# Four weight loads re-timed, one product moved and two statistics handed to ScalarE in a fused attention and expert layer

## The chip, the cores and the metric

The kernel runs on one core of a Trainium2 chip. The metric is the time of one execution in microseconds (us) on the device; lower is better. A core has TensorE (PE, with its weight loads shown apart as PEld), VectorE (DVE), ScalarE (ACT), GpSimd (POOL) and SyncE (SP), which run their own instruction streams and wait for each other by semaphores, and 16 DMA engines that SP and POOL feed here.

## The reference

Input `x` is 4 sequences of 1024 tokens with 256 features, float32. The layer is attention and then a routed feed-forward, each on a normalized input and added to its own input:

```python
qkv = layernorm(x) @ qkv_w.T + qkv_b            # 16 heads of 16, rope on q and k
attn = softmax(causal(q k^T / 4)); x = x + (attn @ v) @ proj_w.T + proj_b
z = layernorm(x)
aff = z @ centroids.T; e = argmax(aff)          # 8 experts, top 1 for each token
ye = z + relu(layernorm_e(z) @ w1[e].T + b1[e]) @ w2[e].T + b2[e]
alpha = sigmoid(aff[e]); x = x + alpha * ye + (1 - alpha) * z
```

Each expert has a first weight matrix of 1024 x 256 and a second of 256 x 1024, 1 MB each.

## The kernel before

The program has three stages.

**Projection** (0 to about 120 us) makes q, k and v and writes q and k as bfloat16 parts to DRAM (`qk_parts`).

**Attention** (about 120 to 523 us) runs in 16 steps, n = 0 to 15, one for each group of four heads of a sequence (`NQ`), and a short tail. In step n, PE computes the scores and products of group n (L1252, L1269) and, between them at hand-written places (`ITEM_AT`, `PV_AT`), 18 "items" of group n+1 (L1145, L1156), from which DVE takes block maxima (L1009). The first item of a step (`item == 0`) waits until the whole stack of q and k of its group is in SBUF: 14 DMAs, `STACK_LOADS`, which SP issues in `load_stack` (L387, L392, L396, L401) for group n+2 in the second half of step n, and which are complete on one semaphore. Ahead of them in each step, in SP's program order, SP stores the inverted softmax sums of an earlier group (`store_inverse`, L228), places an output (`place_out`, L213, L217), sends the maxima (L744) and spreads inverted sums (`spread_inverse`, L235). In step 5, 7 and 9 it then stores three pad rows. Once in some steps, at sub-step `W2_AT = 4`, POOL issues one load of 1 MB from its own queue: the second weights of one of the first `LOADED = 6` experts (L824). `early_at` says in which step each goes.

**Route and experts** (from 523 us). For `NP = 16` pairs of token tiles PE projects the attention output (L2049, L2053), DVE adds the residual and keeps the logits (`add`, L1673, L1674), and mean and variance of the pair are taken either by DVE (`stats` of DVE, L1683, L1686) or by ACT (`stats` of ACT, L1564, L1568, L1570), as `BY_ACT` says. Pairs are grouped (`GROUPS`); per group DVE finds the expert (`one_hot`), PE makes ranks (`rank_products`), DVE makes row positions (`positions`, `row_scalars`), and POOL scatters the rows of the group's tiles to DRAM by one indirect DMA for each tile (L1506). After group 3 the first slot table is made. SP, in its own order, loads x, the columns and the biases, then waits until all attention outputs are normalized (`s_nm`) and loads the second weights of experts 6 and 7 (L1460, 2 MB), then waits for the slot table and loads the first weights of slot 0 (L246), then waits for the scatters of groups 0 to 3 (L1465) and loads the rows of slots 0 and 1 (L344):

```python
for e in range(LOADED, NE):
    if e == OUT_AT_WEIGHTS:
        sp.wait_ge(s_pj, KB)
    if e == INV_AT_WEIGHTS:
        sp.wait_ge(s_nm, NQ // 2)
    sp.dma_start(w2s[:, e * W2C:(e + 1) * W2C], w_exp[e][:, W1C:WCOLS]).then_inc(s_late, 16)
sp.wait_ge(s_tab, 2)
load_w1(sp, Step(0))
```

The attention outputs are normalized in 8 products of 128x1024 (`normalize_out`, L242): six on POOL, two on DVE. The last of them is in DVE's pair loop. PE waits for it before pair 12. Then 39 slots (32 full, 7 of half size) follow, each a hidden layer (L2075) and an output (L2099); the first needs its rows normalized by ACT (L1557) and turned by PE (L1996), the register loads of three slots (L1426) and the projection of pair 15, which PE does between them.

Of the kernel before, what the change touches and what calls it, by code (L numbers as in the profile page):

```python
# [45 lines left out]
FIRST_GROUPS = 4  # L46
# [84 lines left out]
def program(nc, x, x_feat, w_qkv, b_qk, b_val, w_proj, w_proj_out, b_proj, cent, w_exp, cols, b2, consts, rope, out):  # L131
    ctx = ExitStack()
    with ctx:
# [229 lines left out]
        def wait_rows(eng, S):  # L363
# [3 lines left out]
            else:  # L367
                wait_dma(eng, s_rl, S)

        phase_route_experts(nc, x, pay_d, load_w1, load_rows, load_half_rows, row_data, row_scalar, wait_rows, w2s, w1b, s_w1, cols, b2, cst, ident, eps, slot_tab, col, b2r,  # L370
                            wp, bp3, ones3, xl, o_feat, arena[:, spare:NE * WCOLS], arena[:, spare - 2 * W2C:spare], s_b3, out, gate,
                            o_late[:, 0, :], w_exp, s_late, s_nm, place_out, invert_sums, store_inverse, spread_inverse, normalize_out)
# [34 lines left out]
def phase_project_attend(nc, x, x_feat, w_qkv, b_qk, consts, rope, parts_d, w_exp, s_w, arena, v_all, spare, cst, ident, eps,  # L407
# [5 lines left out]
    with ExitStack() as ctx:  # L413
# [238 lines left out]
        def wait_free(eng, i, item, alone=None):  # L652
            wait(eng, s_free, i, ITEMS, number(i, item) + 1, alone)

        early_at = (1, 2, 3, 4, 5, 14)
        W2_AT = 4
        assert len(early_at) == LOADED
        BY_POOL = NQ // 2 - 2
# [630 lines left out]
def phase_route_experts(nc, x, pay_d, load_w1, load_rows, load_half_rows, row_data, row_scalar, wait_rows, w2s, w1b, s_w1, cols, b2, cst, ident, eps, slot_tab, col, b2r,  # L1289
# [3 lines left out]
    with ExitStack() as ctx:  # L1293
# [12 lines left out]
        starts = [sum(GROUPS[:g]) for g in range(NG + 1)]  # L1306
        FIRST = GROUPS[:FIRST_GROUPS]
        FT = sum(FIRST)
        BY_ACT = range(1, 2 * FIRST_GROUPS, 2)

        def pairs_by(act, u):

            return sum((m in BY_ACT) == act for m in range(u))

# [113 lines left out]
        def expert_of(eng, S, known):  # L1428

            if S.reg is not None:  # L1430
                return expert(eng, S)
            if S.const not in known:
                known[S.const] = expert(eng, S)
            return known[S.const]
# [5 lines left out]
        with nc.Block() as block:  # L1440
# [99 lines left out]
            def _(act):  # L1540
                known = {}

                def roots(g):
                    act.wait_ge(s_v, 2 * pairs_by(False, starts[g + 1] // 2))
                    act.wait_ge(s_va, 5 * pairs_by(True, starts[g + 1] // 2))
                    act.activation(sd[:, 0, of(g)], mv[:, of(g), 1], ACT.Sqrt, bias=eps).then_inc(s_sd, 1)
                    if g == 0:
                        act.wait_ge(s_pre, 6)
                    act.activation(sd[:, 1, of(g)], mv[:, of(g), 1], ACT.Sqrt, bias=eps2[:, :], scale=1.0 + EPS).then_inc(s_sd, 1)
# [10 lines left out]
                def stats(u):  # L1560
                    before = pairs_by(True, u)
                    act.wait_ge(s_x2, u + 1)
                    for t in (2 * u, 2 * u + 1):
                        act.activation(junk[:, t % 2, :], xr[:, t, 0:DIM], ACT.Copy, scale=1.0 / (HD * DIM),  # L1564
                                       accum_out=am[:, t:t + 1]).then_inc(s_va, 1)
                    act.wait_ge(s_va, 5 * before + 2)
                    for t in (2 * u, 2 * u + 1):
                        act.activation(junk[:, 2 + t % 2, :], xr[:, t, 0:DIM], ACT.Square, bias=am[:, t:t + 1], scale=-1.0 / HD,  # L1568
                                       accum_out=mv[:, t, 1:2]).then_inc(s_va, 1)
                    act.activation(mv[:, 2 * u:2 * u + 2, 0], am[:, 2 * u:2 * u + 2], ACT.Copy, scale=float(HD)).then_inc(s_va, 1)  # L1570

                for w in range(NP):
# [4 lines left out]
                    for g in range(NG - 2):  # L1577
                        if w == starts[g + 1] // 2 + (1 if g < FIRST_GROUPS else 3):
                            roots(g)
                    if w in BY_ACT:  # L1580
                        stats(w)
# [69 lines left out]
            def _(dve):  # L1651
# [15 lines left out]
                def add(u):  # L1667
                    n, at = 2 * u + 1, 2 * u % R
                    two = xr[:, n - 1:n + 1, 0:DIM]
                    dve.wait_ge(s_pj, n + 1)  # L1670
                    last = 2 * n // G >= len(s_x) - 1
                    dve.wait_ge(s_x[-1] if last else s_x[2 * n // G], 32 if last else 16)
                    dve.tensor_tensor(two, ps_p[:, at:at + 2, 0:DIM], two, ALU.add).then_inc(s_x2, 1)  # L1673
                    dve.tensor_tensor(xl[:, n - 1:n + 1, :], ps_p[:, at:at + 2, DIM:DIM + NE], xl[:, n - 1:n + 1, :],  # L1674
                                      ALU.add).then_inc(s_lg, 1)

                def stats(u):
                    before = 2 * pairs_by(False, u)
                    dve.wait_ge(s_x2, u + 1)
                    if before >= R:  # L1680
                        dve.wait_ge(s_v, before + 2 - R)
                    for i in range(2):
                        dve.bn_stats(st[:, (before + i) % R, :], xr[:, 2 * u + i, 0:DIM]).then_inc(s_bn, 1)  # L1683
                    for i in range(2):
                        dve.wait_ge(s_bn, before + i + 1)
                        dve.bn_aggr(mv[:, 2 * u + i, :], st[:, (before + i) % R, :]).then_inc(s_v, 1)  # L1686
# [21 lines left out]
                def positions(g):  # L1708
                    r, k = g % 2, GROUPS[g]
                    dve.wait_ge(s_rk, g + 1)  # L1710
                    dve.wait_ge(s_sn, g)
                    dve.tensor_tensor(rank[:, 0:k, :], ps_k[:, 0:k, :], seen[:, :].unsqueeze(1).to_broadcast([P, k, NE]),
                                      ALU.add).then_inc(s_rc, 1)
                    dve.wait_ge(s_rc, 3 * g + 1)
                    dve.tensor_tensor(seen[:, :], ps_k[:, G, :], seen[:, :], ALU.add).then_inc(s_sn, 1)
                    dve.tensor_tensor(mine[:, 0:k, :], rank[:, 0:k, :], hot[:, r, 0:k, :], ALU.mult).then_inc(s_rc, 1)
                    dve.wait_ge(s_rc, 3 * g + 2)
                    dve.tensor_reduce(posf[:, 0:k], mine[:, 0:k, :], AX.X, ALU.add).then_inc(s_rc, 1)
                    dve.wait_ge(s_rc, 3 * g + 3)
                    dve.tensor_copy(posi[:, of(g)], posf[:, 0:k]).then_inc(s_ps, 1)  # L1720

                def row_scalars(g):
                    dve.wait_ge(s_sd, 2 * (g + 1))
                    dve.reciprocal(sd[:, 2, of(g)], sd[:, 0, of(g)]).then_inc(s_rs, 1)
                    dve.reciprocal(xr[:, of(g), COL_S], sd[:, 1, of(g)]).then_inc(s_sb, 1)
                    dve.wait_ge(s_rs, g + 1)
                    dve.tensor_tensor(xr[:, of(g), COL_K], sd[:, 1, of(g)], sd[:, 2, of(g)], ALU.mult).then_inc(s_sb, 1)
                    dve.tensor_tensor(xr[:, of(g), COL_GATE], top[:, of(g)], sd[:, 2, of(g)], ALU.mult).then_inc(s_sb, 1)
                    dve.wait_ge(s_sb, 4 * g + 1)
                    dve.scalar_tensor_tensor(out=xr[:, of(g), COL_B], in0=mv[:, of(g), 0], scalar=-1.0, in1=xr[:, of(g), COL_S],  # L1730
                                             op0=ALU.mult, op1=ALU.mult).then_inc(s_sb, 1)
# [112 lines left out]
                for u in range(NP):  # L1844
                    add(u)
                    if u == 2:
                        invert_sums(dve, NQ - 1)
                    if u == 7:
                        normalize_out(dve, NQ // 2 - 1)
                    if u % 2 == 0 and 2 <= u <= 2 * FIRST_GROUPS:  # L1850
                        positions(u // 2 - 1)
                        row_scalars(u // 2 - 1)
                    if u % 2 == 1 and u < 2 * FIRST_GROUPS:
                        one_hot(u // 2)
                    if u < 2 * FIRST_GROUPS and u not in BY_ACT:
                        stats(u)
                    if u == 2 * FIRST_GROUPS:
                        first_table()
                    if u > 2 * FIRST_GROUPS:
                        stats(u - 1)  # L1860
                    if u == starts[FIRST_GROUPS + 1] // 2:
                        one_hot(FIRST_GROUPS)
                    if u in (2 * FIRST_GROUPS + 2, 2 * FIRST_GROUPS + 4):
                        dve.wait_ge(s_tab, 2)
                        expert_of(dve, Step(u // 2 - FIRST_GROUPS - 1), known)
                    if u == starts[FIRST_GROUPS + 1] // 2 + 2:
                        positions(FIRST_GROUPS)
                        row_scalars(FIRST_GROUPS)
                    if u == starts[FIRST_GROUPS + 2] // 2:
                        one_hot(FIRST_GROUPS + 1)  # L1870
# [310 lines left out]
```

## Time and profile before

| | |
|---|---|
| median of 3 runs | 867.91 us (865.54 to 869.71) |
| profiled execution, its own time | 862.7 us |
| its span | 861.0 us |
| PE busy | 805.0 us (93%) |
| DVE busy | 594.6 us (69%) |
| ACT busy | 517.0 us (60%) |
| POOL busy | 340.4 us (40%) |
| mean DMA rate | 150 GB/s |

The span is what the profiler saw from the first instruction to the last. The profiled execution was 5.2 us shorter than the median of the timed ones.

### The profile page before, as it was taken

Reading aid. Unit: us, or ns where it says so; the run is one execution under the profiler, and the core shown is the slowest. Engines: PE = TensorE matmul, PEld = TensorE weight load, DVE = VectorE, ACT = ScalarE, POOL = GpSimd, SP = SyncE. Lnnn points to the kernel's source line nnn. Section 1 sums busy time; section 2 is a strip of 40 time slices with the busy share of each in tenths; the row PEclk is TensorE's granted clock in tenths of the full one; section 3 lists DMA queues with packets and bytes.
Section 4 is the critical chain, followed back from the end, with each engine's and each line's share of the span. In section 5 each row is a group of like instructions: output and inputs, shape, how many; then the busy total and the mean of one; then the engine's idle time right before and its main releaser. Section 6 shows DMA issues by size and latency. Waiting matters only on the chain. (4 is left out here: it accounts for less than half of the span.)

```text
span 861.0 us, 24382 instructions
## 1 busy us (share of the span) xinstructions
PE 805.0 (93%) x8788; PEld 494.0 (57%) x8789; DVE 594.6 (69%) x1145; ACT 517.0 (60%) x1211; POOL 340.4 (40%) x476
## 2 busy tenths in 40 slices
PE   6999868999998999999999988877999999999994
PEld 4555433444343444443444434566999999999873
DVE  5878999999898999999999704764733333333353
ACT  4668335888787888888888894223333333333351
POOL 9999672443242434334343432634111111143211
PEclk9999988999999999999999999899999999999998
DMA  8578632445447343343334315866555555556550
GB/s 289 165 240 252 200 111 76 132 126 112 120 99 163 95 115 102 86 109 84 82 90 97 76 43 174 273 218 206 182 185 185 182 182 180 183 191 194 178 207 4
DMA packets 63354, 128.90 MB, mean 150 GB/s; under 512 B 16981, under 2 KB 44246, under 8 KB 56982
## 3 DMA queue, kind: packets, MB, share of 16 engines
q1 hardware_dynamic: 59094, 112.53, 44.5%
q0 software_dynamic: 4160, 15.03, 5.3%
q8 instruction: 64, 1.05, 0.5%
q14 instruction: 36, 0.29, 0.1%
HBM read 99.89 MB, written 22.98 MB: 143 GB/s over the span
## 5 line engine op out<-in xcount | busy, mean ns | idle before, releaser
L929 ACT ACTIVATE arena<-ps_pair 128x512 f32<-128x512 f32 (+2 forms) x640 | 317.9, 557 | 64.6 <-PE ps_pair L1252 61.8
L1009 DVE TENSOR_REDUCE B_block_max<-ps_item 128x8 f32<-128x1024 f32 x288 | 335.4, 1217 | 28.2 <-PE ps_item L1156 27.8
L1252 PE MATMUL ps_pair<-q_stack,k_stack 99*32 99x512 bf16 (+7 forms) x3072 | 197.5, 331 | 2.7 <-ACT arena L929 1.8
L843 POOL TENSOR_SCALAR_AFFINE_SELECT arena<-arena 128x256 f32<-128x256 f32 x256 | 102.1, 408 | 153.3 <-ACT arena L929 151.2
L1269 PE MATMUL ps_pair<-arena,B_v_quad 128*32 128x512 f32 (+3 forms) x1536 | 155.9, 487 | 1.2 <-ACT B_oacc L948 0.7
L1252 PEld LDWEIGHTS ps_pair<-q_stack,k_stack 99*32 99x32 bf16 (+1 forms) x3072 | 69.0, 95 | 119.7 <-ACT arena L929 60.8
L2099 PE MATMUL C_ps_p<-arena 128*128 x512 | 118.0, 382 | 4.4 <-issue 4.4
L2075 PEld LDWEIGHTS C_bank<-arena 128*128 128x128 f32 x1024 | 120.3, 193 | 2.5 <-ACT arena L1595 0.6
L2075 PE MATMUL C_bank<-arena 128*128 128x128 f32 x1024 | 120.7, 277 | 0.4 <-ACT arena L1625 0.4
L1156 PE MATMUL ps_item<-k_stack,q_stack 64*128 64x128 bf16 (+2 forms) x1280 | 107.3, 265 | 14.7 <-DVE B_block_max L1009 8.9
L1625 ACT ACTIVATE arena<-C_bank,ffn_columns 128x128 f32<-128x128 f32 x128 | 36.5, 367 | 121.9 <-PE C_bank L2075 109.8
L2099 PEld LDWEIGHTS C_ps_p<-arena 128*128 128x128 f32 x512 | 95.2, 191 | 17.6 <-issue 6.0
L1532 POOL DMA_INDIRECT out<-C_res,C_ids x32 | 31.8, 993 | 180.6 <-issue 125.8
L1156 PEld LDWEIGHTS ps_item<-k_stack,q_stack 64*128 64x128 bf16 x1280 | 45.5, 94 | 86.5 <-DVE B_block_max L1009 43.9
L1926 DVE TENSOR_SCALAR arena<-C_bank,ffn_columns 128x128 f32<-128x128 f32 x128 | 36.0, 345 | 79.0 <-PE C_bank L2075 67.2
L1269 PEld LDWEIGHTS ps_pair<-arena,B_v_quad 128*32 128x32 f32 x1536 | 42.5, 109 | 28.5 <-issue 11.5
L1196 PE MATMUL ps_pair<-arena 128*128 128x512 f32 x128 | 58.3, 598 | 0.0
L780 POOL TENSOR_TENSOR arena<-arena 128x512 f32<-128x512 f32 x32 | 51.1, 1608 | 5.6 <-DVE arena L1050 5.2
L1595 ACT ACTIVATE arena<-C_bank,ffn_columns 128x128 f32<-128x128 f32 (+1 forms) x78 | 30.8, 445 | 35.4 <-PE C_bank L1996 34.5
L1906 DVE TENSOR_TENSOR C_y<-C_ps_p,ffn_bias 128x256 f32<-128x256 f32 x32 | 13.6, 424 | 52.7 <-PE C_ps_p L2099 52.6
L1050 DVE SCALAR_TENSOR_TENSOR arena<-ps_pair,A_bq,arena 128x512 f32<-128x512 f32 x64 | 44.5, 742 | 7.6 <-PE ps_pair L1196 7.5
L1506 POOL DMA_INDIRECT payload<-C_x_rows,C_posi x32 | 31.5, 986 | 41.8 <-issue 29.3
(213 smaller groups left out, 781.0 us busy)
## 6 DMA issues: line engine op xcount, KB each, us to landing
arena<-in_w_exp SPq DMA_DIRECT2D x41, 1024.0 KB
qk_parts<-arena SPq DMA_DIRECT2D x32, 384.0 KB, 3.5
q_stack<-qk_parts SPq DMA_DIRECT2D x96, 128.0 KB, 3.5
k_stack<-qk_parts SPq DMA_DIRECT2D x64, 128.0 KB, 3.5
arena<-in_w_exp POOLq DMA_DIRECT2D x6, 1024.0 KB, 7.0
rows<-payload SPq DMA_DIRECT2D x32, 130.5 KB, 2.1
arena<-in_x SPq DMA_DIRECT2D x8, 512.0 KB, 4.7
arena<-in_x_feat SPq DMA_DIRECT2D x8, 512.0 KB, 5.6
```

The source lines that it names most:

```text
L780: pool.tensor_tensor(rot[:, h % 2, c, :], rot[:, h % 2, c, :], ds[:, h % 2, 1 - c, :], op).then_inc(s_rot, 1)
L843: pool.affine_select(out=block_p, in_=block_p, compare_op=ALU.is_ge, fill=0.0, base=0, pattern=[[0, 2], [1, P]], channel_multiplier=-1).th ...
L929: act.activation(pr[s % PR][:, h:h + 2 * n - 1:2, 0:W], ps_s[(EXPS * Q.const + exps_to[s] + u) % R][:, 0:n * W].rearrange("p (h n) -> p h ...
L1009: dve.tensor_reduce(bmx[:, g:QH:GH, first:first + 3 * gap + 1:gap], src[:, :, :].rearrange("p c (b n) -> p c b n", n=P), AX.X, ALU.max).th ...
L1050: dve.scalar_tensor_tensor(out=out[:, h % 2, at, :], in0=ps_qk[h % 2][:, c, :], scalar=bq[:, n:n + 1], in1=rp[:, table, positions(h)], op0 ...
L1156: mm = pe.matmul(dst[:, half, at * P:(at + n) * P], qs[rows, r, half, bass.ds(g * SEQ + t * P, P)], ks[rows, r, half, bass.ds(g * SEQ + kb ...
L1196: mm = pe.matmul(ps_qk[h % 2][:, c, :], wq[:, k, at:at + P], z[:, g % 2, k, :], start=(k == 0), stop=(k == DC - 1))
L1252: mm = pe.matmul(bank[at:at + 32, :], ks[rows, r, half, bass.ds(g * SEQ + kb * P + at, 32)], qs[rows, r, half, bass.ds(g * SEQ + c * QW + ...
L1269: mm = pe.matmul(ps_o[32 * h:32 * h + 32, off:QW], vq[:, r, kb, h, :], pr[s % PR][:, h, 0:QW - off], start=(kb == 0), stop=(kb == 4 * c + ...
L1625: act.activation(hr[:, S.ring(2), c, :], ps_h[0][:, c, :], ACT.Relu, bias=col[:, bass.ds(e, 1), 2 * DC + c]).then_inc(s_r[0], 1)
L2075: mm = pe.matmul(ps_h[f // HC][:, f % HC, :], w1b[:, S.ring(W1R), at:at + P], xT[:, r, c, :], start=(c == 0), stop=(c == DC - 1))
L2099: mm = pe.matmul(ps_y[r], hr[:, r, c, :], w2s[:, bass.ds(e * W2C + c * DIM, DIM)], start=(c == 0), stop=(c == FC - 1))
```

## The change

It has three parts. `early_at` moves the loads of the second weights of experts 2, 3 and 4 from steps 3, 4 and 5 to steps 4, 6 and 8 (experts 0, 1 and 5 stay in steps 1, 2 and 14). The last `normalize_out` on DVE moves from behind the add of pair 7 to behind that of pair 9. The statistics of pairs 9 and 11 move from DVE to ACT.

```diff
-        early_at = (1, 2, 3, 4, 5, 14)
+        early_at = (1, 2, 4, 6, 8, 14)
...
-        BY_ACT = range(1, 2 * FIRST_GROUPS, 2)
+        BY_ACT = range(1, 2 * FIRST_GROUPS + 4, 2)
...
-                    if u == 7:
+                    if u == 9:
                         normalize_out(dve, NQ // 2 - 1)
...
                     if u > 2 * FIRST_GROUPS:
-                        stats(u - 1)
+                        if u - 1 not in BY_ACT:
+                            stats(u - 1)
```

On POOL, in steps 3 and 4 of attention (L798 begins a step's values, L824 is the load of 1 MB, L843 the causal masks, L242 a normalization), the order before is:

```order
L798 COPY B_v_quad<-arena 128x32x16
L829 CAST B_n<-B_nr 96x128
L831 TENSOR_TENSOR B_n<-B_n,cst 96x128
L834 TENSOR_TENSOR B_nm<-B_n,B_nr 96x128
L843 AFFINE_SELECT arena<-arena 128x2x128 x4
L824 DMA arena<-in_w_exp 128x2048
L843 AFFINE_SELECT arena<-arena 128x2x128 x12
```

In the changed kernel the same place of step 3 reads as follows, and the rows above come one step later:

```order
L798 COPY B_v_quad<-arena 128x32x16
L829 CAST B_n<-B_nr 96x128
L831 TENSOR_TENSOR B_n<-B_n,cst 96x128
L834 TENSOR_TENSOR B_nm<-B_n,B_nr 96x128
L843 AFFINE_SELECT arena<-arena 128x2x128 x16
```

Step 3 has lost its load; steps 5 and 7 have none either, and steps 4, 6 and 8 have one each, ahead of 12 masks and of the normalization that stands in each of these steps.

On DVE, between the add of pair 7 (L1673, L1674) and the expert choice of group 3 (L1696 and on), this is the difference:

```order
 L1673 TENSOR_TENSOR C_x_rows<-C_ps_p,C_x_rows 128x2x256
 L1674 TENSOR_TENSOR x_logits<-C_ps_p,x_logits 128x16
-L242 TENSOR_TENSOR arena<-arena 128x1024
 L1696 TENSOR_REDUCE C_top<-x_logits 128x4
 L1698 TENSOR_TENSOR C_ge<-x_logits,C_top 128x32
```

The product is gone from there. Behind the first slot table, from the add of pair 9 to the add of pair 11, DVE in the changed kernel has:

```order
L1770 TENSOR_TENSOR slot_tab<-C_es,cst 1x8
L1673 TENSOR_TENSOR C_x_rows<-C_ps_p,C_x_rows 128x2x256
L1674 TENSOR_TENSOR x_logits<-C_ps_p,x_logits 128x16
L242 TENSOR_TENSOR arena<-arena 128x1024
L1683 BN_STATS C_st<-C_x_rows 128x6 x2
L1686 BN_AGGR C_mv<-C_st 128x2 x2
L1673 TENSOR_TENSOR C_x_rows<-C_ps_p,C_x_rows 128x2x256
L1674 TENSOR_TENSOR x_logits<-C_ps_p,x_logits 128x16
L1426 TENSOR_LOAD slot_tab
```

The product now follows the slot table and the add of pair 9; the four statistics instructions that stood ahead of L1426 (pair 9) are on ACT, and so are those of pair 11.

## Rows read from the trace of the kernel before

**Rows 1.** One line's instructions (the transposed maxima, once a step), PE, three stretches
```profile
L1132 PE MATMUL ps_item<-cst,B_mx x2: 314/314/314, 198.1 to 225.0; 128*96 128x128 f32 x2
L1132 PE MATMUL ps_item<-cst,B_mx x2: 313/314/315, 248.9 to 276.6; 128*96 128x128 f32 x2
L1132 PE MATMUL ps_item<-cst,B_mx x7: 313/314/315, 324.4 to 467.8; 128*96 128x128 f32 x7
```

**Rows 2.** Timeline of PE, steps 4 to 6: start, duration, [idle before]
```profile
222.57 0.61 PE L1156 MATMUL ps_item<-k_stack,q_stack 64*128 64x512 bf16 x4 [1.74 <-DMA k_stack<-qk_parts]
...
266.16 0.38 PE L1156 MATMUL ps_item<-k_stack,q_stack 64*128 64x128 bf16 x7 [1.79 <-issue]
...
274.20 0.60 PE L1156 MATMUL ps_item<-k_stack,q_stack 64*128 64x512 bf16 x4 [1.94 <-DMA k_stack<-qk_parts]
```

**Rows 3.** Stack loads to next first item, steps 2 to 7: stretch, busy, clock, DMA share, GB/s
```profile
182.80:195.70 12.90, 12.90 (x242) 6.22 (x236) 12.33 (x12) 11.01 (x24) 5.33 (x14) 1.00 0.74 206
206.60:219.50 12.90, 12.65 (x216) 5.75 (x212) 11.21 (x11) 9.74 (x21) 4.95 (x13) 1.00 0.97 212
233.40:246.30 12.90, 12.90 (x246) 6.13 (x234) 12.33 (x12) 11.02 (x24) 7.31 (x14) 1.00 0.76 212
257.30:270.20 12.90, 11.11 (x204) 5.09 (x192) 10.64 (x10) 9.28 (x20) 5.03 (x13) 1.00 0.96 204
285.10:298.00 12.90, 12.90 (x242) 6.21 (x236) 12.33 (x12) 11.01 (x24) 7.23 (x14) 1.00 0.41 128
309.00:321.90 12.90, 12.90 (x242) 6.20 (x236) 12.32 (x12) 11.01 (x24) 4.91 (x13) 1.00 0.64 168
```

**Rows 4.** Last stack loads of step 4, its time to landing, and the next first item
```profile
L401 SPq DMA_DIRECT2D k_stack<-qk_parts x2: 637/980/1323, 242.3 to 243.7; - x2
DMA to landing us min/median/max: 2.3/2.7/3.1
...
246.29 0.61 PE L1156 MATMUL ps_item<-k_stack,q_stack 64*128 64x512 bf16 x4
```

**Rows 5.** The same three of step 6
```profile
L401 SPq DMA_DIRECT2D k_stack<-qk_parts x2: 589/590/591, 295.0 to 295.6; - x2
DMA to landing us min/median/max: 2.2/2.4/2.5
...
297.92 0.60 PE L1156 MATMUL ps_item<-k_stack,q_stack 64*128 64x512 bf16 x4
```

**Rows 6.** Timeline of the route stage, DVE, SP, ACT and PE
```profile
550.95 1.22 DVE L242 TENSOR_TENSOR arena<-arena 128x1024 f32<-128x1024 f32 x1
...
552.20 0.80 SPq L1460 DMA_DIRECT2D arena<-in_w_exp  x2
...
558.89 0.01 SPq L246 DMA_DIRECT2D arena<-in_w_exp  x1
...
561.87 0.69 DVE L1673 TENSOR_TENSOR C_x_rows<-C_ps_p,C_x_rows 128x512 f32<-128x512 f32 x1 [1.41 <-PE C_ps_p L2053]
...
562.56 0.74 DVE L1683 BATCH_NORM_STATS2 C_st<-C_x_rows 128x6 f32<-128x256 f32 x2
...
563.56 0.30 ACT L1546 ACTIVATE C_sd<-C_mv,eps 128x6 f32<-128x6 f32 x1 [9.87 <-DVE C_mv L1686]
...
566.95 1.44 SPq L344 DMA_DIRECT2D rows<-payload  x2
...
569.05 0.60 ACT L1557 ACTIVATE arena<-rows 128x256 f32<-128x256 f32 x1 [5.01 <-DMA rows<-payload]
...
572.07 0.39 PE L2049 MATMUL C_ps_p<-b_proj_rows,ones_rows 3*128 3x264 bf16 x2 [1.86 <-issue]
```

**Rows 7.** The last four scatters ahead of slot 0, POOL: durations, first and last start
```profile
L1506 POOL DMA_INDIRECT payload<-C_x_rows,C_posi x4: 956/960/1003, 555.9 to 559.7; - x4
```

**Rows 8.** Busy times in stretches of the route stage, columns as in rows 3
```profile
559.00:564.00 5.00, 5.00 (x23) 3.42 (x23) 3.52 (x15) 0.44 (x2) 1.35 (x2) 1.00 1.01 346
564.00:569.00 5.00, 3.69 (x23) 2.54 (x21) 4.31 (x19) 0.05 (x1) 0.00 (x0) 1.00 0.27 93
```

## The prediction

> **What bounds the kernel now.** I read the windows of attention first, because two of the three edits can only act where an engine that sets the pace waits. In a step of attention PE is busy for the whole stretch shown, 12.90 of 12.90 us, with DVE at 12.3 [rows 3]: PE sets the period. Then I looked for steps that are longer than others. The transposed maxima stand once in each step, so their distance is the period: (467.8 - 324.4) / 6 = 23.9 us in the late steps, but 26.9 us from 198.1 to 225.0 and 27.7 us from 248.9 to 276.6 [rows 1]. These two steps lose 3.0 + 3.8 = 6.8 us. PE's timeline says where: 1.74 us at 222.57 and 1.94 us at 274.20, both for a stack DMA in front of the first item of steps 4 and 6, and 1.79 us at 266.16 in the middle of an item, where no semaphore is waited for and only DMA traffic is unusual [rows 2]. The rest of the 6.8 us is the refilling of the pipe behind these holes.
>
> Why these steps? The windows from the start of the stack loads to the next first item show DMA shares of 0.74, 0.97, 0.76, 0.96 in steps 2 to 5, which carry a weight load, and 0.41 and 0.64 in steps 6 and 7, which carry none [rows 3]. So an odd step is about 0.2 heavier than an even one for nearly the same traffic, a weight load adds 0.33 in either (0.74 - 0.41, 0.97 - 0.64), and only odd plus load reaches 1. The two holes follow exactly the odd steps 3 and 5. Step 4 had its load as well, and the next first item came 246.29 - 222.57 = 23.7 us after its own, without a wait [rows 2, 4].
>
> In the route stage the chain into the experts runs through DMA. SP can load the rows of slot 0 only at 566.95, although the last of the four scatters that it waits for was issued at 559.7 [rows 6, 7]; ACT waits 5.01 us for these rows until 569.05, and PE comes to the last projection at 572.07, behind the turning of these rows and its register loads [rows 6]. The DMA engines are full until 564 (1.01) and nearly idle afterwards (0.27 over 5 us) [rows 8]. DVE is not the bound there: it idles 1.41 us before the add of pair 11, and ACT 9.87 us [rows 6].
>
> **The change part by part.** *Weight loads.* Steps 3 and 5 lose their load. Their share goes to about 0.97 - 0.33 = 0.64, that of step 7, after which PE did not wait. That gives back 3.0 + 3.8 = 6.8 us. Steps 4, 6 and 8 carry a load. For step 4 the row with a load is at hand: last stack DMA issued 243.7, landing 2.3 us later at 246.0, first item at 246.29, 0.3 us to spare [rows 4]. Step 6 without a load had 295.6 + 2.2 = 297.8 against 297.92, 0.1 us to spare [rows 5], so a load there that delays the last landing by as much as the slower one of rows 4 (3.1 against 2.3) would cost up to 0.8 us. Bounds for the three steps together: nothing (as step 4 was) and 3 x 3.0 = 9.0 us (as step 3 was). Their share with a load would be 0.41 + 0.33 = 0.74, which is the even row, so I take a value next to the lower end: 0.5 us in all. The POOL instruction itself takes well under a microsecond of an engine that is busy 7.3 of 12.90 us [rows 3]; nothing waits behind it but masks.
>
> *The last product.* It leaves DVE's path to the slot table, where it took 1.22 us [rows 6]: all of group 3's work can be up to 1.2 us earlier. I cost this at zero gain, because POOL issues its scatters one after another, the last four from 555.9 to 559.7 [rows 7], and their landing is set by full DMA engines. What it delays is SP's queue: behind the wait for this product stand the two loads of 1 MB (552.20), the first weights of slot 0 (558.89) and the rows of slots 0 and 1 (566.95) [rows 6]. The new end of the product: the slot table was ready about 1.5 us before 558.89 and comes up to 1.2 us earlier, so about 556.2; the add of pair 9 takes 0.7, the product 1.2, so 558.2. The 2 MB start 6.0 us later, and the first weights at about 560.5. From there 3 MB at 346 GB/s [rows 8] take 9.1 us, to 567.3, plus what scatters take in between; before, the same queue was done at about 564 + 0.27 x 5 = 565.4. The scatters gain what the loads lose: from about 554 to 558 they have the engines alone. So the rows may be asked for somewhat earlier than 566.95, but they stand behind 3 MB in SP's queue and land at about 568.5 to 570.5 instead of 569.0. Bounds: -1.2 us (the product's own time, if the scatters were all) and +6.0 us (the whole delay). I take +0.6, near the point where both effects meet, since the engines do the same work in all and only stand idle for about 4 us, half of which scatters fill.
>
> The Trainium skill (DMA: Bandwidth & Descriptors, Queues, rings and completion order) says that each DMA engine takes turns between queues packet by packet, and that what one sequencer issues is consumed in its own order. The trace agrees as far as it goes: the rows' DMA, issued after the weights' share has fallen to 0.27, takes 2.1 us to 569.05 [rows 6, 8]. By that rule alone, with the rows strictly behind 3 MB, the sum would have about +2 us in this place; that case is a rival below.
>
> *PE's wait for the product.* Pair 12 waits for it. DVE still waited for PE's earlier pair at 561.87 [rows 6], 3.7 us after the new end, so this wait stays hidden.
>
> *Statistics.* Pair 11's instructions start at 562.56 and free ACT's root at 563.56, so a pair is 1.0 us of DVE; two pairs are 2.0 us [rows 6]. They are hidden before and after: DVE idles 1.41 us there. On ACT the pairs fall into 9.87 us of idle [rows 6]; even at three times DVE's price both fit. If ACT were late, the roots of group 4 would be, then DVE's row scalars and POOL's fifth group of scatters, which no slot before the ninth needs. Bounds: -2.0 to +1; value 0.
>
> **Sum**, against the profiled execution's own 862.7 us: -6.8 + 0.5 + 0.6 + 0 = -5.7, so 857.0. That execution stands 5.2 us under the median of the timed runs; I carry the difference over to the median: 867.91 - 5.7 = **862.2 us**. About 0.5% (4.3 us) is what a measurement of this kernel can tell from no change, so the forecast is only just outside it.
>
> **Rivals.**
>
> *The rows of slot 0 come late (about 865).* The 2 MB and the first weights serialize in front of the rows on SP's queue. For it: SP's order, and a DMA share of 1.01 with no room. Against: group 3's scatters get the hole. Price +2 to +5 instead of +0.6: 863.6 to 866.6.
>
> *The margin in even steps is used up (about 865).* Step 6 had 0.1 us to spare even without a load [rows 5]. If one of the three steps costs as step 3 did, 3.0 us: 865. Against: rows 4.
>
> *Slower: parity is not the cause.* It could be that a load hurts wherever the spread of inverted sums stands right ahead of it, and that step 4 was spared only because the hole before it had given SP time. Then steps 4, 6 and 8, now undisturbed, each cost 3.0 to 3.8 us: 9.0 to 11.4 against the 6.8 given back, plus 0.6, so 870.7 to 873.1. It is slower by over 0.5% from 3.5 us a step on. The Trainium skill (the same page, Issuing engines are not separate DMA queues) holds that all DMAs run on the same 16 engines whoever issues them, by which a megabyte costs the same in any step; that is this case if nothing else differed. Against it: 0.41 and 0.64 in two steps without any weight load [rows 3].
>
> *More than forecast (about 859).* PE's idle times in the route stage shrink as well, if they come from the crowd of loads and scatters; -3 us.
>
> **How the numbers follow.** Forecast 0.50 (own range 860.5 to 864.5), late rows 0.20, margin 0.12, slower 0.06, more 0.12. Below 863.6 lie about 0.40 of the forecast's half, all of "more" and a little of the two middle cases: 0.56 faster. Over 872.2 lies most of "slower": 0.04. The rest, 0.40, is within 0.5%. The range leaves out the tail of "more", the whole of "slower" and the tail of late rows: 858.8 to 868.5.
>
> **What would show it.** Right: the maxima are 23.9 us apart from step 2 on; no idle of PE for a stack DMA after steps 3 and 5; shares of about 0.64 in steps 3 and 5 and 0.74 in 4, 6 and 8. Product at about 557, the two loads at about 558.2 minus the shift of 6.3, rows of slot 0 within 1.5 us of where they were relative to the start of the stage. Wrong: PE waits for stack DMAs after steps 4, 6 or 8, or ACT's wait for the rows of slot 0 grows past 6.5 us; or the unprofiled runs, which are 5.2 us longer than the profiled one, lose their time somewhere that this trace does not show.

## The result and the profile after

The changed kernel takes 873.75 us (median of 6 runs, 872.15 to 877.13) against 866.82 us for the kernel before (median of 6 runs on the same chip). The ratio is 1.0075, with a 95% interval of 1.0048 to 1.0102: slower by 0.75%, where I had forecast 862.2 us and a gain. The profiled execution is the longest of the six, with 877.13 us of its own time and a span of 875.4 us, so it is read for places and mechanisms, and sizes are taken from the timed ratios.

The page of the changed kernel, first lines and clock:

```profile
span 875.4 us, 24390 instructions
PE 812.7 (93%) x8788; PEld 497.5 (57%) x8789; DVE 593.3 (68%) x1137; ACT 522.3 (60%) x1229; POOL 341.7 (39%) x476
PEclk9999978999989999999999999899899999999998
```

PE does the same 8788 matmuls in 7.7 us more busy time, so part of them ran at a lower clock (shown in the last section). The transposed maxima, once a step, as in [rows 1] (of each row, the first and last start us are read):

```profile
L1132 PE MATMUL ps_item<-cst,B_mx x2: 313/313/313, 199.9 to 223.8; 128*96 128x128 f32 x2
...
L1132 PE MATMUL ps_item<-cst,B_mx x2: 312/312/313, 223.8 to 253.3; 128*96 128x128 f32 x2
...
L1132 PE MATMUL ps_item<-cst,B_mx x2: 313/382/450, 277.2 to 305.8; 128*96 128x128 f32 x2
...
L1132 PE MATMUL ps_item<-cst,B_mx x2: 313/314/314, 329.9 to 358.0; 128*96 128x128 f32 x2
```

Steps 3 and 5, which lost 3.0 and 3.8 us before, take 23.9 us. But steps 4, 6 and 8, which now carry the loads, take 29.5, 28.6 and 28.1 us: 5.6 + 4.7 + 4.2 = 14.5 us lost against 6.8. PE's timeline, as in [rows 2]:

```profile
242.20 0.29 PE L1252 MATMUL ps_pair<-q_stack,k_stack 128*32 128x128 bf16 x3 [2.54 <-issue]
...
293.30 0.23 PE L1156 MATMUL ps_item<-k_stack,q_stack 64*128 64x128 bf16 x2 [0.96 <-issue]
...
302.00 0.60 PE L1156 MATMUL ps_item<-k_stack,q_stack 64*128 64x512 bf16 x4 [2.31 <-DMA k_stack<-qk_parts]
...
354.00 1.04 PE L1156 MATMUL ps_item<-k_stack,q_stack 64*128 64x512 bf16 x4 [2.73 <-DMA k_stack<-qk_parts]
```

They are the two kinds of holes that steps 3 and 5 had: the stack of the next group late, and PE without an instruction in the middle of a group. The windows from the start of the stack loads, steps 3 to 8, columns as in [rows 3]:

```profile
208.40:221.30 12.90, 12.90 (x242) 6.16 (x236) 12.33 (x12) 11.02 (x24) 4.97 (x13) 1.00 0.56 138
232.30:245.20 12.90, 10.36 (x168) 4.83 (x160) 8.58 (x8) 7.29 (x17) 4.17 (x12) 0.85 0.97 201
261.80:274.70 12.90, 12.90 (x242) 6.19 (x236) 12.32 (x12) 11.01 (x24) 4.94 (x13) 1.00 0.69 164
285.80:298.70 12.90, 11.94 (x224) 5.74 (x220) 11.22 (x11) 9.98 (x22) 7.05 (x13) 1.00 1.02 204
314.50:327.40 12.90, 12.90 (x242) 6.22 (x236) 12.33 (x12) 11.02 (x24) 4.92 (x13) 1.00 0.49 155
338.40:351.30 12.90, 12.87 (x240) 6.12 (x232) 12.33 (x12) 11.02 (x24) 7.26 (x14) 1.00 0.97 211
```

I had forecast 0.74 for steps 4, 6 and 8. They show 0.97, 1.02 and 0.97 at no more GB/s than the 212 of step 4 before: the DMA engines are busy longer for the same bytes. The DMA queues of step 4, 13 us from the start of its stack loads, show it directly. q0 is POOL's queue, which carries only the weights, and q1 is SP's; the columns are packets, MB and the share of the 16 engines' time. The first two rows are of the changed kernel (232 to 245), the next two of the kernel before (233.4 to 246.4):

```profile
q1 hardware_dynamic: 532, 1.51, 60.3%
q0 software_dynamic: 144, 1.05, 34.5%
```
```profile
q1 hardware_dynamic: 630, 1.65, 49.9%
q0 software_dynamic: 144, 1.05, 24.2%
```

The same 1.05 MB took 34.5% of the engines' time instead of 24.2%. The load of this step landed 12.0 us after its issue, against 6.8 us in step 4 before.

### The profile page after: what moved, and what is told of

Same layout as the page of the kernel before. It is cut to its first block and busy times, and to the rows that moved or that the text cites. A ratio compares the mean times of both kernels' runs of the same rounds, so it can differ in the third digit from the quotient of the medians.

```text
span 875.4 us, 24390 instructions
## 1 busy us (share of the span) xinstructions
PE 812.7 (93%) x8788; PEld 497.5 (57%) x8789; DVE 593.3 (68%) x1137; ACT 522.3 (60%) x1229; POOL 341.7 (39%) x476
## 3 DMA queue, kind: packets, MB, share of 16 engines
q8 instruction: 64, 1.05, 0.5%
## 5 line engine op out<-in xcount | busy, mean ns | idle before, releaser
L1009 DVE TENSOR_REDUCE B_block_max<-ps_item 128x8 f32<-128x1024 f32 x288 | 335.3, 1217 | 33.7 <-PE ps_item L1156 33.4
L843 POOL TENSOR_SCALAR_AFFINE_SELECT arena<-arena 128x256 f32<-128x256 f32 x256 | 102.9, 411 | 154.7 <-ACT arena L929 152.7
L1269 PE MATMUL ps_pair<-arena,B_v_quad 128*32 128x512 f32 (+3 forms) x1536 | 157.9, 495 | 0.9 <-ACT B_oacc L948 0.7
```

The costliest lines, as they stand in the source:

```text
L843: pool.affine_select(out=block_p, in_=block_p, compare_op=ALU.is_ge, fill=0.0, base=0, pattern=[[0, 2], [1, P]], channel_multiplier=-1).th ...
L1009: dve.tensor_reduce(bmx[:, g:QH:GH, first:first + 3 * gap + 1:gap], src[:, :, :].rearrange("p c (b n) -> p c b n", n=P), AX.X, ALU.max).th ...
L1269: mm = pe.matmul(ps_o[32 * h:32 * h + 32, off:QW], vq[:, r, kb, h, :], pr[s % PR][:, h, 0:QW - off], start=(kb == 0), stop=(kb == 4 * c + ...
```

## The experiments

A step's *loss* below is the distance of its transposed maxima to the next, less 23.9 us. Theories: **meeting**, a load of 1 MB makes a hole when it meets the spread of inverted sums in the DMA engines; **any load**, each load costs in any step from 3 on; **parity**, mine.

### The change taken apart

One kernel has only the new `early_at`, one only the two edits of the route stage, and one only the product.

```diff
-        early_at = (1, 2, 3, 4, 5, 14)
+        early_at = (1, 2, 4, 6, 8, 14)
```

> Only early_at changes, to steps 1, 2, 4, 6, 8, 14. If the three loads in even steps are the loss (5.6, 4.7 and 4.2 us in the changed kernel's trace, against 3.0 and 3.8 us in steps 3 and 5 before), attention is 7 to 8 us longer than before and the time is about 874 us, all of the difference. If the delayed product in the route stage is the loss, this kernel is at or under the time before, 861 to 867 us.

Measured: 874.06 us, ratio 1.0071 (1.0047 to 1.0095). Its steps 4, 6 and 8 lose 5.0, 3.5 and 6.2 us. By itself this one line costs as much as the whole change (1.0071 against 1.0075). The route stage adds a little of its own, as the next two runs show, and the intervals leave room for both.

> Only the product behind the add of pair 9 and the statistics of pairs 9 and 11 on ACT; early_at as before. If the loads in attention are the whole loss: 866 to 868 us, no change that can be measured. If the late 2 MB in SP's queue cost what the row of the delay says (rows of slot 0 2.3 us later after the start of the stage), about 869.

Measured: 869.74 us, ratio 1.0019 (1.0001 to 1.0038), a cost of 0.1 to 3.3 us. It fits the second case, with the late 2 MB, better than the first.

```diff
-                    if u == 7:
+                    if u == 9:
                         normalize_out(dve, NQ // 2 - 1)
```

> Only the last product moved from behind the add of pair 7 to behind that of pair 9. Forecast of the step in my sum: +0.6 us, 867.4 to 869.5. If the rows of slot 0 are as late as 2.3 us after the start of the stage: +2 us, about 869.5. If the whole +0.2% of the two route edits lies in the statistics: no change.

Measured: 870.25 us, ratio 1.0027 (1.0009 to 1.0045). The late product costs about 0.8 to 3.9 us by itself. Whether the statistics take some of it back can't be told from 1.0019 and 1.0027.

### Where in its step the load stands

`W2_AT` moves POOL's load along its step. These four differ from the kernel before in that number alone.

```diff
-        W2_AT = 4
+        W2_AT = 2
```

> The kernel before with W2_AT = 2: POOL issues each weight load about 5 us earlier in its step, right behind the maxima's last part, so that its 1 MB is over when the stack loads begin, while it still meets the spread of inverted sums. If the meeting with the stack loads makes the holes: both are gone, maxima 23.9 us apart in steps 3 and 5, -6.8 us, about 860.5 us. If the meeting with the spread makes them: holes of 3 to 4 us stay, 866 to 868 us.

Measured: 861.07 us, ratio 0.9927 (0.9905 to 0.9949). The loads go out 2.3 us into their step, steps 3 and 4 take 23.9 us, and step 5 loses 0.6. All six loads (L824) land in less than 6 us, before the first stack loads go out at 8.5 us of the step, and the windows of steps 3 to 5 show 0.62, 0.54 and 0.71:

```profile
L824 POOL DMA_DIRECT2D arena<-in_w_exp x6: 593/593/772, 153.1 to 464.7; - x6
DMA to landing us min/median/max: 5.3/5.5/5.7
```
```profile
207.14:220.04 12.90, 12.90 (x242) 6.20 (x236) 12.32 (x12) 11.02 (x24) 4.93 (x13) 1.00 0.62 140
231.04:243.94 12.90, 12.90 (x242) 6.20 (x236) 12.32 (x12) 11.01 (x24) 7.27 (x14) 1.00 0.54 144
254.94:267.84 12.90, 12.88 (x240) 6.11 (x232) 12.32 (x12) 11.01 (x24) 4.93 (x13) 1.00 0.71 166
```

> The kernel before with W2_AT = 3: each load goes out at about 5.5 us of its step, 0.8 to 1 us ahead of the spread instead of 1 to 1.5 us behind it, and 3 us ahead of the stack loads. If closeness of load and spread in either order makes the holes: 3 to 5 us in steps 3 and 5 stay, 866 to 869 us. If it is load and spread being still under way when the stack loads begin, a load that is 2 us earlier loses less: 1 to 2 us a step, 863 to 865 us. If a load must only not be queued behind a spread: none, 861 us.

Measured: 871.74 us, ratio 1.0052 (1.0021 to 1.0084): worse than before, which none of my three cases said. The loads go out at 5.4 us, land fast (5.4 to 7.0 us), and steps 3, 4 and 5 lose 2.4, 6.3 and 4.1 us. The waits are of another kind:

```profile
211.42 0.40 PE L1252 MATMUL ps_pair<-q_stack,k_stack 99*32 99x512 bf16 x4 [2.22 <-DMA q_stack<-B_nm]
...
239.04 0.62 PE L1252 MATMUL ps_pair<-q_stack,k_stack 99*32 99x512 bf16 x4 [3.54 <-DMA q_stack<-B_nm]
...
268.00 0.40 PE L1252 MATMUL ps_pair<-q_stack,k_stack 99*32 99x512 bf16 x4 [2.35 <-DMA q_stack<-B_nm]
```

B_nm are the maxima that SP sends (L744) in two transfers, here at 4.3 to 5.2 and 5.2 to 6.0 us of the step, so close around the load. The scores wait for them. The semaphore events show them late: the second one is complete 5.9, 6.8 and 6.5 us after its issue in steps 3 to 5, against 2.3 us in the kernel before. With `W2_AT = 2` it took 5.2 and 5.1 us in steps 1 and 2, where the maxima go out within a microsecond of the load and no spread is sent, and 2.8 to 3.0 us in steps 3 to 5, where they go out 2.3 to 3.6 us behind it. So a load makes a small transfer beside it late, and one that is a few microseconds ahead does it little harm; in steps 1 and 2 PE lost nothing, since these maxima left early in the step.

> The kernel before with W2_AT = 6: each load goes out at about 10 us of its step, 3.6 us or more behind the spread, and in the middle of the stack loads. If the distance from the spread alone decides (2.9 us were enough in step 4): no holes, about 861 us. If the sum of traffic up to the next step decides: the last stack loads land later than now, holes of 4 us and more in steps 3 to 5, and in 1 and 2 as well, over 870 us.

Measured: 870.23 us, ratio 1.0028 (1.0003 to 1.0052). Its profiled execution was 9 us over its own median, so only the places are read. With the load 10 us into the step, every laden step loses, 1 and 2 too, where there is no spread (4.0, 3.4, 1.1, 2.8 and 5.2 us in steps 1 to 5). The loads of these steps land after 10 to 12 us, beside the stack loads. Distance from the spread alone does not decide.

> The kernel before with W2_AT = 1: the weight load goes out some 3 to 5 us ahead of a step's start, beside the last stack loads of the step before, and is over before the spread. If what matters is that load, spread and the first stack loads do not meet: no holes, about 861 us, as with W2_AT = 2. If any meeting with stack loads costs: the last stack loads land late and holes of 1 to 3 us stand behind steps 2 to 4, 864 to 869 us.

Measured: 867.58 us, ratio 0.9985 (0.9965 to 1.0005). The profiled execution took 870.02 us. The loads go out 18 to 21 us into the step before. Steps 1 and 2 lose 5.6 and 5.0 us, the next ones nothing:

```profile
178.24 0.61 PE L1156 MATMUL ps_item<-k_stack,q_stack 64*128 64x512 bf16 x4 [4.27 <-DMA k_stack<-qk_parts]
```

In steps 1 and 2 the load went out 0.5 and 0.3 us ahead of the last stack load, which then landed 6.9 and 5.6 us after its issue, together with the megabyte. In steps 3 and 4 it went out 1.3 and 1.7 us behind it, and the stack was in time. These two holes lose 10.6 us against 6.8 in the profile before, while the time is not longer; this stays open, and the profile is read for places only.

### Which step, and what went before

```diff
+        early_at = (1, 2, 6, 7, 8, 14)
```

> The kernel before with early_at = (1, 2, 6, 7, 8, 14), two even steps around an odd one, W2_AT = 4. If each load costs 4 to 5.6 us in any step that has a spread: 3 holes, 13 to 15 us lost against 6.8 before, about 874 to 876 us. If a step behind a hole is spared because the hole has given SP time to send the spread earlier (as step 4 before): holes in 6 and 8 alone, about 9 to 10 us lost, 869 to 871 us. If parity were the cause: step 7 alone, about 864 us.

Measured: 869.29 us, ratio 1.0020 (0.9992 to 1.0047). Steps 6, 7 and 8 lose 2.7, 0.0 and 4.6 us. The odd one between two even ones is spared, and parity falls by this run alone. SP sent the spread (L235) of steps 6, 7 and 8 at 276.06, 301.28 and 327.12, and POOL's load went out at 277.6, 304.3 and 328.2: 1.6, 3.0 and 1.1 us later. In step 4 before it was 2.9 us. The likely reason is the hole in front, which gave SP time to place an output before the step began: its maxima and its spread go out 1 to 2 us earlier in it than in the other steps. I put the laden steps of all runs with `W2_AT = 4` side by side, from the issue times and semaphore events of their traces (the kernel with the spread sent first, whose holes are another wait, and step 14, which has no stack loads, are left out):

```
spread to load, us   load lands after, us   loss of the step, us   steps
no spread            5.4 to 6.4             0.0 to 0.7             1 and 2 of every run
2.9 to 3.2           6.2 to 6.8             0.0 to 0.2             4 before, 7 here, 4 of two more
2.4                  9.2                    1.5                    4 of the product-only kernel
0.75 to 1.6          10.8 to 13.5           2.7 to 6.2             19 steps of 8 kernels
```

Both exceptions say something. In step 14 the load stands 2.2 us behind the spread and lands after 6.0 to 7.7 us: without stack loads the meeting costs it little. With the spread sent first, the loads of steps 3 to 5 went out 2.7 to 2.9 us behind it and landed after 8.4 to 9.2 us, not 6.2 to 6.8: so distance is not the whole rule.

> The kernel before with the six loads in steps 1, 2, 3, 5, 7, 14 (W2_AT = 4): three laden steps that have a spread ahead of the load, each behind an unladen step. Each loses 3 to 6 us as steps 3 and 5 before and 4, 6 and 8 of the change did: 10 to 14 us against 6.8, 870 to 875 us. If odd steps cost less than even ones: about 869 us.

Measured: 873.62 us, ratio 1.0063 (1.0034 to 1.0092); steps 3, 5 and 7 lose 3.3, 3.4 and 3.7 us. Odd steps undisturbed by a hole lose as even ones do.

### The spread taken away, and doubled

Loads in odd steps as above; the spreads of steps 3, 5 and 7 are sent one step later, two at once.

```diff
+                    if n.const in (4, 6, 8):
+                        spread_inverse(sp, n.const - 4)
-                    if n.const >= 3:
+                    if n.const >= 3 and n.const not in (3, 5, 7):
                         spread_inverse(sp, n.const - 3)
```

> As the kernel with loads in steps 1, 2, 3, 5, 7, 14, but the spreads of steps 3, 5 and 7 are sent one step later, two in steps 4, 6 and 8, which have no load. If the meeting of spread and load is the cause: no hole in 3, 5 and 7, 10 to 14 us less than with the spreads in place, 861 to 864 us with 0 to 1 us for a step with two spreads. If the load and the stack loads alone make the holes in steps from 3 on: 3 to 6 us a step stay, 870 to 875 us.

Measured: 884.71 us, ratio 1.0204 (1.0154 to 1.0254). The total missed my number by over 20 us, and the reason is the finding. Steps 3, 5 and 7, with a load and without a spread, lose 0.0, 0.0 and 0.6 us; all loads (L826 here) land within 6.6 us. Steps 4, 6 and 8, with two spreads and no load at all, lose 9.5, 5.4 and 8.0 us. The loads, PE's wait behind step 4, and the windows of steps 3, 4 and 5:

```profile
L826 POOL DMA_DIRECT2D arena<-in_w_exp x6: 593/593/772, 157.9 to 492.5; - x6
DMA to landing us min/median/max: 5.7/6.0/6.6
```
```profile
251.49 1.03 PE L1158 MATMUL ps_item<-k_stack,q_stack 64*128 64x512 bf16 x4 [7.54 <-DMA k_stack<-qk_parts]
```
```profile
207.16:220.06 12.90, 12.90 (x242) 6.21 (x236) 12.32 (x12) 11.03 (x24) 4.92 (x13) 1.00 0.77 206
231.06:243.96 12.90, 12.89 (x240) 6.13 (x232) 12.32 (x12) 11.03 (x24) 4.37 (x12) 1.00 0.88 138
264.51:277.41 12.90, 12.90 (x242) 6.20 (x236) 12.32 (x12) 11.03 (x24) 4.93 (x13) 1.00 0.84 225
```

Two spreads keep the engines 0.88 busy at 138 GB/s; a weight load without a spread, with the same stack loads, 0.77 at 206 GB/s in step 3 (step 5, with 0.84 at 225, has the pad rows too). The spread reads four rows of 4 KB sixteen times each, 256 KB in all. For its bytes it is the dearest transfer of a step. So the meeting is the cause: neither step number nor load alone makes a hole at this place. The two spreads show that a hole needs no load either: a second spread does in its place. How one transfer slows the other in the engines was not tested.

> The kernel before (steps 1, 2, 3, 4, 5, 14, W2_AT = 4) with one order changed on SP: the spread of inverted sums is issued ahead of the sending of the maxima, so it goes out 1.6 to 2 us earlier, at 3.7 to 5 us of a step where the spared steps 4 (4.57) and 7 (4.48) had it. If a hole comes from a spread that goes out within 1.5 us of the weight load: holes 3 and 5 gone or under 1 us, about 862 us. If the stack loads alone decide: holes stay, 867 to 869 us.

Measured: 902.72 us, ratio 1.0404 (1.0373 to 1.0436). The spread went out 1.7 us earlier, as meant, but the maxima were now behind it in SP's queue, and steps wait for them, laden or not:

```profile
PE ps_pair L1252 <- DMA q_stack<-B_nm: 17.6, 5, 7.1
```

That is 17.6 us in five waits over steps 3 to 7, the longest 7.1 us. The run could not settle its question. It shows that a transfer of a few KB behind a spread is late: the maxima are complete 4.8 to 10.1 us after the second one's issue in steps 3 to 8, against 2.3.

### The route stage, and better kernels

> The product behind pair 9, with the weight loads of attention as before, and SP's order changed: first weights and rows of slot 0 ahead of the 2 MB that wait for the product. The product alone cost 0.27% (0.09 to 0.45). If it costs because slot 0's weights and rows stand behind the late 2 MB: hidden layer of slot 0 about 2.5 to 5 us earlier than with the product alone, 866 to 868 us, unless the first output now waits for the 2 MB. If it costs on DVE or PE: 869 to 871 us as before.

Measured: 868.05 us, ratio 1.0017 (0.9994 to 1.0040); the product alone had 1.0027 (1.0009 to 1.0045), so the times don't separate them. The profiles do in part: ACT has the first rows of slot 0 45.5 us after the stage's first load (L1445), as before (45.7), against 49.6 with the product alone. But then ACT waits 4.74 us for slot 1's rows, which now stand behind the 2 MB. The order on SP is not the only candidate for the product's price: from 500 to 612 us PE waits 7.8 us here for the logits that DVE keeps (L1674), 7.2 us with the product alone, and 2.0 us in the kernel before. Over all profiled kernels it is 6.5 to 7.8 us in the five with the product late and 2.0 to 5.1 us in the twelve with it in its place. Part of it comes ahead of the late product, but each of the five has one wait of 1.9 to 3.1 us that ends about 5 us after the product's start, where the kernel before has none.

> The whole change, with W2_AT = 2 instead of 4. If where a load stands inside its step is the cause and which step it is does not matter: the three holes of 4.2 to 5.6 us go, 873.7 - 14 = about 860 to 863 us, within 2 us of the kernel before with W2_AT = 2 (861.1). If even steps are bad of themselves: over 868 us.

Measured: 861.95 us, ratio 0.9942 (0.9922 to 0.9963). With `W2_AT = 2` the change's own steps lose nothing, as the first case said.

> The kernel before with W2_AT = 2 and the statistics of pairs 9 and 11 on ACT; the product stays behind pair 7. The statistics were costed at nothing (-2.0 to +1): 860 to 862 us, as with W2_AT = 2 alone (861.1).

Measured: 860.27 us, ratio 0.9922 (0.9896 to 0.9948), against 0.9927 with `W2_AT = 2` alone: the statistics on ACT make no difference that can be told.

> What the runs so far point to: loads in steps 1, 2, 4, 6, 8, 14 at W2_AT = 2, statistics of pairs 9 and 11 on ACT, the product where it was. Without the 0.64 us that step 5 lost with a load at W2_AT = 2: 859 to 860.5 us. If the order of steps does not matter any more: 860 to 861 us, as the same with steps 1 to 5 (860.3).

Measured: 861.61 us, ratio 0.9919 (0.9889 to 0.9949). The three kernels with `W2_AT = 2` and the product where it was can't be told apart; each beats both kernels. Loads in even steps bring nothing over steps 1 to 5.

## Why the prediction was wrong

- **What bounds attention.** Right: PE sets the period, and the holes behind steps 3 and 5 are DMA's. They are removed by removing the loads from these steps, as forecast (-6.8 us).
- **Why these steps.** Wrong, and this is the step that failed. "Only odd plus load reaches 1" was read from two even laden steps. Step 2 has no spread at all, and step 4 was no clean sample: it followed a hole, and its spread went out 2.9 us ahead of its load instead of 1.1 and 0.9 as in steps 3 and 5. Even steps behind an unladen one fill the engines as well (0.97, 1.02 and 0.97). What made the holes is the meeting of load, spread and stack loads.
- **The term +0.5 us for steps 4, 6 and 8.** I took the lower end, by step 4. The profile has 14.5 us. The bound of 3 x 3.0 = 9.0 was too low too, since it took the cheaper of the two odd steps and no fall of the clock: after its hole of 2.54 us step 4 has 6.6 us at half clock (below). By time, the weights alone cost 6.2 us (1.0071, interval 4.1 to 8.3); the two profiles give 14.5 - 6.8 = 7.7 us, inside that interval.
- **The rival "parity is not the cause"** had the right mechanism, spread near load, step 4 spared by the hole before it, and 870.7 to 873.1 us, next to the 873.75 measured. It got 0.06, because of 0.41 and 0.64 in two steps without a load. It was partly another thing: step 6 too followed a hole and had its spread 2 us earlier in the step than step 7, and step 7 has the pad rows (128 against 168 GB/s in [rows 3]). A difference between odd and even steps remains, but beside the point: without a load, spreads take 5.8 to 9.2 us to land in odd steps and 5.1 to 6.6 in even ones, and both have room. The Trainium skill (DMA: Bandwidth & Descriptors, Issuing engines are not separate DMA queues) has all DMAs run on the same 16 engines; that a load on POOL's queue is slowed by a spread on SP's agrees with it (24.2% and 34.5% of the engines above). So the megabyte's price is not a constant here.
- **The last product, +0.6 us.** Too small. The late 2 MB and then the late rows came as described, but whether they are the whole price is not shown. SP's, PE's and ACT's rows of the changed kernel, as in [rows 6]:

```profile
533.02 0.40 SPq L1445 DMA_DIRECT2D C_x_rows<-in_x  x1
...
569.92 0.80 SPq L1460 DMA_DIRECT2D arena<-in_w_exp  x2
571.92 0.23 SPq L246 DMA_DIRECT2D arena<-in_w_exp  x1
...
573.63 0.38 PE L2050 MATMUL C_ps_p<-b_proj_rows,ones_rows 3*128 3x264 bf16 x2 [1.94 <-DVE x_logits L1674]
...
578.87 1.44 SPq L344 DMA_DIRECT2D rows<-payload  x2
...
582.35 1.09 ACT L1557 ACTIVATE arena<-rows 128x256 f32<-128x256 f32 x2 [4.79 <-DMA rows<-payload]
```

  The product ran at 568.69, 35.7 us after the stage's first load (I had 33.7: 557.0 less the 523.3 of that load before), the 2 MB went out 8.0 us later in the stage than before (I had 6.0), and the rows landed 3.6 us later: 582.35 - 533.02 = 49.3 against 45.7. Measured by time, 2.3 us for the product alone (0.8 to 3.9). The rival "late rows", +2 to +5, was the better number; its profile price of 3.6 us compares with 2.3 us in the time. PE's longer waits for DVE's logits (6.5 us in the changed kernel, 2.0 before, 500 to 612 us) are a second candidate for the same price, and no run parts the two.
- **PE's wait for the product, statistics.** I had PE's wait hidden. In the profile PE never waits for the product itself, but its waits for the logits grew (above): one of them, 1.94 us at 573.63, follows the product at 568.69. The statistics cost nothing that can be measured (0.9922 with, 0.9927 without, both at `W2_AT = 2`), as costed.
- **The sum.** The two profiled executions differ by 877.13 - 862.7 = 14.4 us: 1.3 ahead of the maxima of step 0, 8.4 from there to the maxima of step 14 (467.8 before), 4.7 from these to the end. The medians differ by 6.9, since a short execution of the old kernel and the longest of the new one were profiled. From the maxima of step 14 to the end, eleven profiled kernels with the product in its place took 393.2 to 399.2 us (mean 396.3; the one whose profiled execution was 9 us over its median is left out), five with it late 397.5 to 400.0 (mean 398.6). The difference, 2.3, is what the time of the product alone gives; the rest of the 4.7 is within the scatter of either group.

## What to carry to other kernels

A step that did not stall in spite of a suspected load is evidence only if the step before it did not stall; look at when its other transfers were issued. Count transfers by the engine time that they take for their bytes, not by their bytes: here a spread of 256 KB took nearly as much as a load of 1 MB (step 3 goes from 0.97 to 0.56 without its load and to 0.77 without its spread; a second spread takes an unladen step 4 from 0.48 to 0.88). A bulk load belongs where nothing with a deadline is issued just behind it or beside it (here, what went out within 1 us of it was late), and that place is found along the step rather than by choosing the step.

## What the hardware showed that I had not expected

- **A small transfer that is slow.** The spread of 256 KB lands 5.1 to 9.2 us after its issue in steps without a load; a weight load of 1 MB at `W2_AT` 2, 3 or 4 in a step without a spread lands after 5.4 to 6.6 us. Two spreads together landed 13 to 15 us after the first was issued. The semaphore events of the kernel before hint at a reason: each weight load and each stack load raises its semaphore 16 times, but a spread 5 times, once 1.0 us after its issue and four times at its landing (210.75 to 211.75 for the one issued at 204.45). That fits a transfer whose 64 packets of 4 KB are carried by four of the 16 engines only. No run varied its form, so this is not shown.
- **A load delays what is issued just behind it to about its own end.** The last stack load 0.5 us behind a megabyte landed after 6.9 us, against 2 to 3 us; PE waited 2.2 to 3.5 us for the maxima beside one. Maxima 2.3 to 3.6 us behind a load were complete after 2.8 to 3.0 us, against 2.3.
- **The clock after a hole.** Windows of the changed kernel behind its holes at 242.20, 302.00 and 354.00:

```profile
240.00:248.00 8.00, 5.80 (x51) 1.81 (x55) 3.53 (x4) 2.79 (x6) 3.65 (x5) 0.59 0.82 163
302.00:306.50 4.50, 4.50 (x33) 1.16 (x33) 2.54 (x3) 2.08 (x4) 0.00 (x0) 0.62 0.35 59
354.00:358.00 4.00, 4.00 (x28) 0.90 (x28) 2.36 (x2) 1.17 (x3) 0.00 (x0) 0.57 0.36 58
```

  PE idled 2.54, 2.31 and 2.73 us ahead of these, and beside them the granted clock fell to 0.50, that is from 2.4 to 1.2 GHz, for 3.4 to 6.6 us (by what is missing from 1.00 in each window, doubled: 3.4, 3.4 and, at 242.20, 6.6). Behind the holes of 1.74 and 1.94 us before, the same window shows 1.00:

```profile
222.60:226.60 4.00, 4.00 (x45) 1.29 (x49) 3.56 (x5) 2.83 (x6) 0.48 (x2) 1.00 0.42 73
274.20:278.20 4.00, 4.00 (x45) 1.28 (x49) 3.53 (x5) 2.81 (x6) 0.45 (x2) 1.00 0.43 75
```

  So a hole in the changed kernel can cost twice its length (step 4 lost 5.6 us for 2.54).
- **PE without an instruction.** At 242.20 PE stops after the first of four equal matmuls and goes on 2.54 us later, with nothing to wait for. The profile has a queue of instruction packets (q8, 64 packets of 16 KB), and one of them ran from 239.01 to 240.60. That PE waited for its own program behind full DMA engines fits all such holes, but it was only argued.
